# Moving the remainders of a weight matrix behind later matrix products at the start of a fused float32 kernel

## The reference, cut to what matters

```
x = x + L0(x)                       # x rounded to 64 levels, step and zero point chosen by |x| among 8 thresholds
x = x + x @ W1[id].T                # W1: 1024x1024, one of 8 chosen by the batch
x = x + x @ W2.T + 0.5*(x @ A.T) @ B.T        # W2: one 1024x1024 for all; A of rank 32 chosen by the batch
x = x + 16/16*(x @ B3.T) @ A3.T     # rank 16, chosen by the batch
```

## Time and profile before

| | |
|---|---|
| device time, median of 3 runs | 485.09 us (484.99 to 485.19) |
| the profiled execution, device time | 486.4 us |
| its span, first to last instruction | 484.6 us |
| PE busy | 465.8 us (96%) |
| DVE busy | 418.6 us (86%) |
| ACT busy | 359.5 us (74%) |
| DMA | 67.07 MB, 138 GB/s in the mean |

### The profile page before, as it was taken

One profiled execution on the slowest core, in us unless ns is written; L12 is line 12 of the kernel. 1 busy time (PEld: TensorE's weight loads), 2 busy tenths in 40 slices (PEclk: granted clock), 3 DMA queues, 4 the chain that ended last, 5 costly groups with the idle time before them and its releaser, 6 DMA issues.

```text
span 484.6 us, 8214 instructions
## 1 busy us (share of the span) xinstructions
PE 465.8 (96%) x3184; PEld 426.1 (88%) x3184; DVE 418.6 (86%) x480; ACT 359.5 (74%) x384; POOL 45.2 (9%) x46
## 2 busy tenths in 40 slices
PE   3999769999999999999999999999999999999997
PEld 3969669899898989899998989899999989899995
DVE  3999999988999899989999899989999899989120
ACT  5989968679787879679787879679787879676011
POOL 1054001200003000200002000200002000100000
PEclk9999979999999999999999999999999999999999
DMA  7997314712236113712326113712336123702002
GB/s 276 402 415 243 131 34 148 292 45 103 90 95 284 43 60 131 276 60 103 106 91 268 44 62 127 287 49 103 118 93 254 43 73 116 289 5 87 1 1 87
DMA packets 17830, 67.07 MB, mean 138 GB/s; under 512 B 2576, under 2 KB 5904, under 8 KB 13712
## 3 DMA queue, kind: packets, MB, share of 16 engines
q1 hardware_dynamic: 17808, 66.81, 37.7%
HBM read 56.84 MB, written 9.96 MB: 138 GB/s over the span
## 4 chain that ended last, share of the span: by engine, by line
PE 83%; DVE 8%; ACT 4%; DMA 2%; issue 1%; POOL 0%; DVEq 0%; SPq 0%; ACTq 0%
PE x_bank L598 45%; PE acc L623 32%; DVE y L460 4%; PE x_bank L611 3%; PE acc L635 2%; PE acc L633 2%; DVE uq L448 1%; ACT tq L329 1%; DMA ua<-w2t 1%; DMA xin<-x 1%; DVE x L473 1%; DVE uq L466 1%; ACT mask L344 1%; DVE tq L439 1%; ACT w2h L400 1%
## 5 line engine op out<-in xcount | busy, mean ns | idle before, releaser
L598 PEld LDWEIGHTS x_bank<-x,w1b 128*128 128x128 f32 x2048 | 234.4, 194 | 8.1 <-issue 4.4
L598 PE MATMUL x_bank<-x,w1b 128*128 128x128 f32 x2048 | 235.8, 277 | 4.0 <-DVE x L473 4.0
L329 ACT ACTIVATE tq<-xin,magic,rdelta 128x1024 f32<-128x1024 f32 x128 | 157.0, 1234 | 3.7 <-DMA xin<-x 3.4
L344 ACT ACTIVATE mask<-absx,negtop 128x1024 bf16<-128x1024 f32 x112 | 128.5, 1147 | 40.8 <-DVE y L460 40.1
L460 DVE COPY_PREDICATED y<-mask,uq 128x1024 f32<-128x1024 int16 x112 | 150.7, 1346 | 0.1
L439 DVE TENSOR_SCALAR tq<-tq,par 128x1024 f32<-128x1024 f32 x128 | 98.5, 769 | 8.5 <-ACT tq L329 4.8
L448 DVE TENSOR_SCALAR uq<-tq,ylow,yhigh 128x1024 f32<-128x1024 f32 x112 | 92.5, 826 | 1.1 <-issue 0.9
L623 PE MATMUL acc<-w2h,x2h 128*128 128x512 f32 x256 | 80.9, 393 | 3.3 <-DVE x2l L479 3.3
L623 PE MATMUL acc<-w2h,x2l 128*128 128x512 f32 x256 | 79.9, 389 | 0.0
L623 PE MATMUL acc<-w2l,x2h 128*128 128x512 f32 x256 | 79.1, 390 | 0.0
L295 POOL TENSOR_TENSOR w1b<-w1b,eye 128x256 f32<-128x256 f32 x32 | 34.6, 1083 | 370.9 <-DMA w1b<-w 370.9
(11 more groups left out here) (56 smaller groups left out, 219.3 us busy)
## 6 DMA issues: line engine op xcount, KB each, us to landing
w1b<-w SPq DMA_DIRECT2D x32, 1024.0 KB, 6.7
xin<-x SPq DMA_DIRECT2D x16, 512.0 KB, 3.7
out<-outb SPq DMA_DIRECT2D x14, 512.0 KB, 2.8
w1b<-w2n SPq DMA_DIRECT2D x4, 1024.0 KB, 10.8
ring<-w2t SPq DMA_DIRECT2D x6, 512.0 KB, 6.3
ua<-e_dram SPq DMA_DIRECT2D x16, 128.0 KB, 2.5
ua<-w2t SPq DMA_DIRECT2D x2, 512.0 KB, 7.2
va<-la SPq DMA_DIRECT2D x8, 128.0 KB, 2.7
```

What stands on the lines that cost most here:

```text
L329: nc.scalar.activation(tq[:, n % TQ, :], flat(xin, c % UN), ACT.Identity, bias=magic[:, 0:1], scale=rdelta[:, g:g + 1]).then_inc(t_ready, 1)
L344: nc.scalar.activation(mask[:, n % MK, :], absx[:, :], ACT.Relu, bias=negtop[:, g:g + 1], scale=1.0).then_inc(mask_ready, 1)
L598: last = nc.tensor.matmul(x2_bank[2 * t + i][:, o % HALF * P:(o % HALF + 1) * P], w1b[:, o, at:at + P], x1[:, t, k, :], start=(o % HALF == ...
```

## The change

Three tables and the order of TensorE's first two batches are rewritten:

- **No remainder in the first 17 steps.** VectorE takes W2's remainders at steps 18, 19, 20, 21, 22, 26, 26, 27, in the order k = 3, 0, 1, 2, 4, 5, 6, 7.
- **Blocks pass the staging buffers in another order.** They come as 4, 5, 6, 7, 0, 1, 2, 3; a buffer is free as soon as ScalarE has rounded the block in it. The remainders of 3, 0, 1, 2 are taken from what stands in the buffers at the end. Blocks 4 to 7 are loaded a second time (4 DMAs of 512 KB more) and get the identity a second time (4 more additions on GpSimd).
- **TensorE, first batch:** only `HIGH` is computed for both units. `LOW` of five blocks (3, 0, 1, 2, 4) for both units comes at the batch's end, behind unit 1's `HIGH`. `LOW` of the other three (5, 6, 7) stands in the second batch, behind six of the eight W1 tiles of unit 2. The U products of the first batch stand there too, in place of behind the third tile.
- **x2 is rounded** one step later for unit 0 (VectorE 14 and 16, ScalarE 15 and 17) and one step earlier for unit 1 (VectorE 20 and 22, ScalarE 21 and 23). All other units keep theirs.
- **SyncE:** the loads of W1 for the second batch and the second loads of W2 are written out, alternating, and no longer wait for VectorE's part of u.

The number of products is the same.

```diff
-        stage = [ua[:, :]] + [ring[:, i, :] for i in range(ST - 1)]
+        stage = [ring[:, i, :] for i in range(ST - 1)] + [ua[:, :]]
+        W2_BLOCK = (4, 5, 6, 7, 0, 1, 2, 3, 4, 5, 6, 7)
+        W2_PLACE = (0, 1, 2, 3, 0, 1, 2, 3, 0, 1, 2, 0)
+        W2_REST = (3, 0, 1, 2, 4, 5, 6, 7)
+        REST_SOON = 5
...
-            def load_w2(k):
-                if k >= ST:
-                    sp.wait_ge(w2l_ready, k - ST + 1)
-                sp.dma_start(stage[k % ST], w2t[k, :, :]).then_inc(stage_in[k % ST], 16)
+            def load_w2(i):
+                if ST <= i < KT:
+                    sp.wait_ge(w2h_ready, i - ST + 1)
+                elif i >= KT:
+                    sp.wait_ge(w2l_ready, i - KT + 2)
+                sp.dma_start(stage[W2_PLACE[i]], w2t[W2_BLOCK[i], :, :]).then_inc(stage_in[W2_PLACE[i]], 16)
...
+            for j in range(PAIRS):
+                sp.wait_ge(w1_used, j + 1)
+                load_w1(a1, j)
+                if j < PAIRS - 1:
+                    load_w2(KT + j)
...
-        ACT_W2, DVE_W2 = (9, 10, 11, 12, 13, 14, 15, 16), (10, 11, 12, 13, 18, 19, 20, 21)
-
-        ACT_X2, DVE_X2 = (14, 16), (13, 15)
+        ACT_W2, DVE_W2 = 9, (18, 19, 20, 21, 22, 26, 26, 27)
+
+        X2_AT = ((14, 16), (12, 14)) + ((13, 15),) * (UN * B - 2)
...
-                    c, off = divmod(n - ACT_X2[i], G)
-                    if off == 0 and 0 <= c < UN * B:
-                        round_x2(c, i)
+                    for c in range(UN * B):
+                        if n == G * c + X2_AT[c][i] + 1:
+                            round_x2(c, i)
...
-                if n in DVE_W2:
-                    k = DVE_W2.index(n)
-                    dve.wait_ge(w2h_ready, k + 1)
-                    nc.vector.tensor_tensor(w2l[:, k, :], stage[k % ST], w2h[:, k, :].bitcast(f32),
-                                            ALU.subtract).then_inc(w2l_ready, 1)
+                for at, k in zip(DVE_W2, W2_REST):
+                    if n == at:
+                        i = len(W2_BLOCK) - 1 - W2_BLOCK[::-1].index(k)
+                        dve.wait_ge(w2h_ready, W2_BLOCK.index(k) + 1)
+                        dve.wait_ge(w2_diag, i + 1)
+                        nc.vector.tensor_tensor(w2l[:, k, :], stage[W2_PLACE[i]], w2h[:, k, :].bitcast(f32),
+                                                ALU.subtract).then_inc(w2l_ready, 1)
...
+            def rest(t, order):
+
+                for i in order:
+                    pe.wait_ge(w2l_ready, i + 1)
+                    product(t, W2_REST[i], LOW)
...
+            def start_batch(b, u_at, second=False):
+
+                pe.wait_ge(x1_ready, UN * b + 1)
+                w1_x1(b, 0, range(u_at))
+                for t in range(UN):
+                    if second:
+                        rest(t, range(REST_SOON, KT))
+                    u_low(b - 1, 2 * t)
+                    u_low(b - 1, 2 * t + 1)
+                w1_x1(b, 0, range(u_at, OT))
...
+            def first_batch():
+                pe.wait_ge(x1_ready, 1)
+                w1_x1(0, 0, range(OT))
+                pe.wait_ge(g_ready, 2)
+                for k in (0, 1, 2, 4, 5, 6, 7, 3):
+                    if k in (0, HALF):
+                        pe.wait_ge(x2l_ready, k // HALF + 1)
+                    pe.wait_ge(w2h_ready, W2_BLOCK.index(k) + 1)
+                    product(0, k, HIGH)
+                pe.wait_ge(e_ready, 2 * EH)
+                second_unit(0, HIGH, first=True)
+                for k in range(HALF, KT):
+                    product(1, k, HIGH)
+                for t in range(UN):
+                    rest(t, range(REST_SOON))
...
+            first_batch()
+            start_batch(1, 6, second=True)
```

More of the change, by code:

```diff
@@ L241, in _, with during @@
                 sp.dma_start(e_dram.rearrange("(h a) r n -> h (a r) n", h=EH)[h], outb[:, h, :]).then_inc(e_out, 16)
+            sp.wait_ge(x1_ready, 2)
+            load_x(1, 1)
             sp.wait_ge(e_out, 16 * EH)
-            sp.wait_ge(w2l_ready, ST + 1)
+            sp.wait_ge(w2l_ready, 1)
             load_u(a0)
-            def during(b, first, second):
+            a1, lab1 = ids_of(1)
+            for j in range(PAIRS):
[3 more added lines that the diff above has]
+                    load_w2(KT + j)
+            sp.wait_ge(vl_ready, 2)
+            load_v(a1, lab1)
+            load_w2(KT + PAIRS - 1)
+            sp.wait_ge(ul_ready, 1)
+            load_u(a1)
+            sp.wait_ge(x1_ready, UN + 1)
+            load_x(2, 0)
+            def during(b, second):
                 a, lab = ids_of(b + 1)
-                if not first:
-                    store(b - 1, 0)
-                    store(b - 1, 1)
+                store(b - 1, 0)
+                store(b - 1, 1)
                 sp.wait_ge(vl_ready, 2 * (b + 1))
@@ L300, in _ @@
                 w2_diagonal(j)
-            for k in range(PAIRS, KT):
-                w2_diagonal(k)
-            with pool.Fori(1, B) as b:
+            for i in range(PAIRS, KT):
+                w2_diagonal(i)
+            for j in range(PAIRS):
+                w1_diagonal(1, j)
+                if j < PAIRS - 1:
+                    w2_diagonal(KT + j)
+            w2_diagonal(KT + PAIRS - 1)
+            with pool.Fori(2, B) as b:
                 for j in range(PAIRS):
@@ L546, in _ @@
                 for i in range(2):
-                    c, off = divmod(n - DVE_X2[i], G)
-                    if off == 0 and 0 <= c < UN * B:
-                        split_x2(c, i)
+                    for c in range(UN * B):
+                        if n == G * c + X2_AT[c][i]:
+                            split_x2(c, i)
                 if 2 <= n < STEPS + 2:
@@ L664, in batch, with second_unit @@
+            def second_unit(b, parts=ALL, first=False, early=HALF):
                 pe.wait_ge(x1_ready, UN * b + 2)
                 w1_x1(b, 1, range(OT))
[L666 to L669, removed]
                 pe.wait_ge(vl_ready, 2 * (b + 1))
@@ L674, in batch, with last_batch @@
                     pe.wait_ge(out_ready, ACCS * b)
[L675 removed]
                 for k in range(early):
[L677 removed]
+                    product(1, k, parts)
                 pe.wait_ge(x2l_ready, BANKS * b + 4)
                 v_x2(range(HALF, KT))
[L680 to L687, removed]
[L688 to L690 removed]
+            def first_batch():
[9 more added lines that the diff above has]
+                second_unit(0, HIGH, first=True)
+                for k in range(HALF, KT):
+                    product(1, k, HIGH)
+                for t in range(UN):
+                    rest(t, range(REST_SOON))
+            def batch(b):
+                start_batch(b, 3)
+                w2_x2(b)
+                second_unit(b)
+                for k in range(HALF, KT):
+                    product(1, k)
+            def last_batch():
+                early = HALF // 2
+                start_batch(LAST, 3)
+                w2_x2(LAST)
+                second_unit(LAST, early=early)
+                for h in range(2):
+                    for k in range(early, KT):
+                        product(1, k, ALL, (h,))
+                    if h == 0:
+                        u_low(LAST, 0)
+                        u_low(LAST, 1)
+                    u_low(LAST, 2 + h)
             bilinear()
@@ L694, in _ @@
             adapters_e()
-            batch(0, first=True)
-            with pe.Fori(1, LAST) as b:
+            first_batch()
+            start_batch(1, 6, second=True)
+            w2_x2(1)
+            second_unit(1)
+            for k in range(HALF, KT):
+                product(1, k)
+            with pe.Fori(2, LAST) as b:
                 batch(b)
-            batch(LAST, last=True)
+            last_batch()
 def kernel(**inputs):
```

52 lines of the change are left out of this document (16 added, 36 removed).

## The result

The changed kernel takes 492.76 us (median of 4 runs, 492.3 to 493.97) where the kernel before, run on the same chip, takes 485.14 (484.99 to 485.48): a ratio of 1.0151, 95% interval 1.0126 to 1.0176. It is slower by 7.3 us (6.1 to 8.5 by the interval's ratios). The forecast was 488.8 us in a range up to 491.4: right in sign, too small in size. One execution of one kernel (under "Both mended") took 599.0 us at a mean granted clock of 0.758 and stands in no ratio.

What follows compares the result with a forecast made beforehand. Only unit 3's x1 was taken to count, with VectorE and ScalarE both full before it. Terms 0 + 1.1 + 0.5 + 0.6 + 1.5 = +3.7 us on the median 485.09 gave 488.8 us, range 485.6 to 491.4.

Steps and rivals of the forecast that it cites:

- What bounds the kernel: First two batches: only when unit 3's x1 is ready counts; some 358 us of TensorE products after it stay unchanged.
- Steps 10 to 13: Four w2l leave VectorE, but ScalarE is full too, so unit 1's x1 moves 0 us (-0.5 to +0.6).
- The fifth w2l: Between unit 1's x1 and unit 2's, VectorE takes five w2l instead of four: +1.1 us.
- TensorE's clock and the earlier x2l: Unit 1: clock falls behind the second x2l wait; VectorE waits at its earlier x2l: +0.5 us (0 to 2.1).
- Loads: Second load of W2's block 4 is ready about when step 22 needs it: counted nothing, up to 1 us if late.
- GpSimd: Four more additions beside VectorE, between about 78 and 94 us, lengthen its instructions: +0.6 us (0 to 1.4).
- The second batch's first unit: From unit 2's x1 to unit 3's, TensorE's twelve extra matmuls decide: 30.2 us instead of 28.7, +1.5 us.
- its list of signs: Expected profile marks, including unit 1's x1 near 67.0, TensorE waiting some 3 us at unit 2, unit 3 near 130.
- The rivals: Faster 483.3 us (0.08), no change 485.2 (0.11), small costs 487.2 (0.18), clock fall 490.4 (0.16), full GpSimd blocking 491.0 (0.06).
- the clock falls at W1·x1: Rival at unit 1: clock falls as before, VectorE waits 2.1 us at its earlier x2l: 490.4 us, chance 0.16.
- its aside, 1 us for block 4: Alternative within the clock-fall rival: VectorE instead waits 1 us for the reloaded block 4.

Runs made afterwards that it cites:

- Both mended: Changed kernel with SyncE's reading of adapter numbers moved earlier and 17 identity matmuls in TensorE's wait for unit 2's x1: 492.17 us, ratio 1.0122.
- the second profile: Profiled execution of a repeat run of the unaltered changed kernel, beside the kernel before: median 492.82 us, ratio 1.0155.

## Why the prediction was wrong in size

Two steps failed. The prediction counted the reload of block 4 as nothing, and VectorE waited 1.1 us for it. And it let TensorE start unit 2 at full clock behind a wait that its own sum made longer: the clock fell there, at 1.5 us. The other terms, together, were off by less than 1 us.

**What bounds the kernel: right.** Only unit 3's x1 counted. It came 5.5 us later, and TensorE's work behind it is the same.

**Steps 10 to 13 (0, measured -0.35 us): right in what it is worth.** 4.5 us less work for VectorE brought unit 1's x1 forward by 0.35 us (0.05 in the second profile), and ScalarE has no gap. VectorE stood idle 5.6 of the 25 us, foretold 4 to 5; 3.71 us of it came at the first x2l, where the working had put it mostly at the second. That ScalarE alone sets unit 1's x1, as the working says, is not shown: relieved, it waited for staging blocks.

**The fifth w2l (+1.1) right. TensorE's clock and the earlier x2l (+0.5, measured about 0.1):** the clock fell where I let it, the five blocks took till 67.5 (68.2 foretold), and ScalarE's x2h was 0.1 us late. The place of the fall was in part luck: in the second profile it fell twice, elsewhere.

**Loads ("I count nothing"): failed.** The wait of 1.08 us was there. I had SyncE issue W1's pair at 71.5 us; reading the adapter numbers held it until 74.9. SyncE does not only issue DMAs, as the opening has it: it also reads two numbers into registers between them. The kernel before shows the same gap at the same reading:

```profile
69.94 0.37 SPq L187 DMA_DIRECT2D ua<-a  x1
74.37 0.36 SPq L190 DMA_DIRECT2D va<-la  x1
```

The transfer itself I had too slow: 9.6 us from W1's issue to the block's use, where it was 7.2 us (74.9 to 82.1). The two errors partly cancel.

**GpSimd (+0.6): near in size, its cause not shown.** The first distance grew by 3.1 us: 1.1 for the w2l, 1.1 for the wait, 0.1 for x2h, and 0.8 left, by which VectorE's other instructions are longer. But the kernel without the four additions has the same 0.8. The 0.34 us that the term rests on was read beside W1's larger addition, and W1's additions stay. So the size was luck, as far as is known.

**The second batch's first unit (+1.5, measured 2.8): failed.** It held the twelve matmuls and what of VectorE's waits they leave; that was right, 1.3 us with the clock up (30.0 against 28.7 us), and 1.2 by leaving the twelve out. The missing 1.5 us is the clock. The prediction had a wait of some 3 us for unit 2's x1 in its list of signs, and had let the clock fall behind waits of 3.75 and 4.0 us, yet went on at full speed behind this one. It was 4.87 us. How long a wait it takes the rows don't tell: the clock stayed up behind 3.27 us in the kernel before, and fell at the end of one of 2.4 us in the changed kernel's second profile.

**The profiled execution against the medians.** To unit 3 the sum should have been 5.5 and not 3.7. The medians are further apart, 7.6 us against 5.9 between the profiled executions, because the one of before (486.4 us) was 1.3 above its median. I took the difference to carry over unchanged. What made that execution longer stays open. The low clock in its first batch is not shown to: in one series runs at a mean granted clock of 0.996 took 485.1 to 485.6 us and those at 0.993 mostly more, but in another the two longest, 488.5 and 489.1 us, were at 0.996, and with the clock up all through (the waits of the kernel before filled) the runs scattered as widely.

**The rivals.** None came true as a whole. The one that the clock falls at W1·x1 came nearest in kind, with the wrong unit; its aside, 1 us for block 4, is what happened.

## What to carry to other kernels

Moving work off a busy engine gains only what its partner has idle: two in-order engines that feed each other, both above 95% busy, must be relieved together, and even that gains only what the next in line leaves: here, with ScalarE relieved as well, W2's staging blocks stood behind both. When a sum makes a wait longer, ask again what TensorE's clock does behind that wait, each time. And work that stands inside a wait is free there: before moving it to a tidier place, look what it will be in front of.

## What was not expected of the hardware

Reading two adapter numbers into SyncE's registers put some 4 us between two DMAs (70.4 to 74.9 us), and moving it ahead of a long wait hid it wholly (70.44 to 70.98). Filling TensorE's wait for unit 2's x1 kept the clock up (1.00 through unit 2's start, against 0.54 and 0.61), but keeping the clock up in the kernel before was worth no more than can be measured.
